# Softmax maximum and sum across partitions: by VectorE in blocks of 32 and one short product each, in place of TensorE transposes

## The chip, the cores and the metric

The kernel runs on one core of a Trainium2 chip. The metric is the device time of the whole kernel in microseconds, lower is better. The four compute engines of the core are named as in the profile: PE (TensorE, matrix products and transposes), DVE (VectorE), ACT (ScalarE) and POOL (GpSimd). Each takes its instructions in order from a queue of its own, and they meet at semaphores. SP (SyncE) issues most of the DMAs.

## The reference, cut to what matters

The kernel computes one post-norm transformer layer in fp32: latent attention over 2048 tokens with 16 heads and a causal mask, then a linear layer, each followed by a layer norm.

```
q     = rms_norm(x @ w_qa.T) @ w_qb.T        # 16 heads, 128 + 64 (rotary)
ckv   = x @ w_kva.T                          # one latent key of 128 + 64 rotary
scores = (q . k) * scale, causal mask
attn  = softmax(scores)                      # max and sum over the keys
x     = layernorm(x + (attn @ v) @ w_o.T)
out   = layernorm(x + (x @ (w * scale).T + bias))
```

## The kernel before

A first phase prepares keys, values and weights (the rows up to about 150 us of the profile). The second phase is the attention, and it is where the change lies.

The 16 heads are worked in four groups of 4 heads, and the 2048 queries in 16 tiles of 128. One iteration `it` is one query tile of one group, so there are 64 iterations. Iteration `it` runs over `keys(it)` = 1 to 16 key tiles, since the mask is causal: 544 steps (it, t) in all, 8.5 on average. One step holds 128 keys on the partitions and 4 heads x 128 queries = 512 columns. So the keys lie across the partitions, and the maximum and the sum over the keys have to cross them.

A step does this, by engine:

- PE `scores`: 5 products of 512 columns into one of two score banks in PSUM (L1464).
- DVE `masked` (t = 0, L1847) or ACT `copy_scores` (L1606) and DVE `max_of` (L1858): the scores go to a slot of a ring in SBUF, the running maximum over the steps to `top`, in SBUF.
- When the iteration's steps are through, the maximum crosses the partitions: PE `turn_max` (4 transposes of 128x128, L1473), DVE `reduce_max` (L1866), PE `spread_max` (4 transposes of a broadcast column, L1484) into the bank `MAXES`.
- DVE `shift` (L1873) subtracts the maximum, ACT `exp` (L1611), ACT `hi` (L1618) rounds to a first part, POOL `values_lo` (L1730) makes the rest, and PE `values` multiplies by the values (3 products, L1494, L1495, L1497).
- DVE `add_up` adds the exponentials into the bank `TOTAL` in PSUM: a copy at t = 0 (L1882, 64 times), an addition otherwise (L1885, 480 times). Then ACT `copy_sum` (L1630), PE `turn_sum` (4 transposes, L1505), DVE `reduce_sum` (L1889) and a reciprocal (L1892), PE `spread_sum` (4 transposes, L1513), DVE `normalise` (L1897).
- ACT `o_hi` (L1636), POOL `o_lo` (L1735), PE `project_out` (step `y`, 12 products, L1527), DVE `add_y` (L1836).

Beside that, each of 32 pairs of iterations has three groups of 18 products of 256 columns: `q` twice (L1427) and `pe` once (L1440), with readers `q_hi`, `q_lo` (L1589, L1829), `rope` (L1808, L1812) and `round_pe` (POOL L1703, L1709), and the DMAs `store_pe` and `load_pe` on SP. PE's results for `q`, `pe`, `y`, the turns and `spread_sum` share three banks in rotation (`aux`).

The order of work is written out ahead by `plan()`: `timetable()` gives every step a slot number and a phase in it, the steps are sorted, `waits_for` pulls prerequisites forward, and every engine runs its part of that one list in order. A slot is one key step, with 13 phases. `scores` of step n come in slot n, its `values` in slot v = `value_slot`, at least 6 slots after the last score of the iteration. In the last quarter of the steps the FFN's steps are mixed in (POOL L1747 to L1768, PE L1535, L1547, DVE L1902 to L1941).

Of the kernel before, what the change touches and what calls it, by code (L numbers as in the profile page):

```python
# [662 lines left out]
N_SCORES, N_AUX = 2, 3  # L663
# [105 lines left out]

def timetable():  # L770

    for it in range(N_ITER):
        for t in range(keys(it)):
            n, v = number(it, t), value_slot(it, t)
            yield n, SCORES_AT, ("scores", it, t)
            yield n, MAX, ("max", it, t)
            yield v - 3, SHIFT, ("shift", it, t)
            yield v - 2, EXP, ("exp", it, t)
            yield v - 1, ROUND, ("hi", it, t)
            yield v - 1, ROUND, ("sum", it, t)  # L780
            yield v - 1, ROUND, ("lo", it, t)
            yield v, VALUES, ("values", it, t)
        e = last_value(it)
        yield last_slot(it) + 1, USE_AT, ("turn_max", it)
        yield value_slot(it, 0) - 3, SPREAD, ("spread_max", it)
        yield e, COPIES, ("copy_sum", it)
        yield e + 1, COPIES, ("copy_out", it)
        yield e, USE_AT, ("turn_sum", it)
        yield e + 3, USE_AT, ("spread_sum", it)
        yield e + 5, USE_AT, ("y", it)  # L790
    for s in range(-2, N_PAIR):
# [3 lines left out]
        for j, use in enumerate(uses):  # L795
            at = window_slot(s, j) if s or use[0] == "pe" else -1
            if s == -1 and use[0] == "pe":
                at = 4
            yield at, USE_AT, use
            if use[0] == "pe":  # L800
                late = 3
                yield at + late, READ, ("round_pe", s + 2)
                yield at + late + 1, READ, ("store_pe", s + 2)
                yield max(at + late + 2, FIRST[2 * s + 2] if s >= 0 else at + 5), READ, ("load_pe", s + 2)


def ffn_timetable():
# [3 lines left out]
    for u in range(NT):  # L811
# [6 lines left out]
        yield n + 1, FFN_TURN, ("turn", u)  # L818
        yield n + 2, FFN, ("scale", u)
        yield n + 3, FFN, ("add_bias", u)  # L820
        yield n + 4, FFN_LINEAR, ("linear", u)
        yield n + 5, MAX, ("z_statistics", u)
# [5 lines left out]
def readers(use):  # L828
# [9 lines left out]
    if use[0] == "turn_max":  # L838
        return [("reduce_max", use[1])]
    if use[0] == "turn_sum":  # L840
        return [("reduce_sum", use[1])]
    if use[0] == "spread_sum":
        return [("normalise", use[1]), ("o_hi", use[1]), ("o_lo", use[1])]
# [15 lines left out]

def waits_for(step):  # L860
# [9 lines left out]
    elif what == "max":  # L870
        yield ("scores", it, *rest)
        if number(it, *rest) >= RING:
            yield ("lo", *previous(it, *rest, RING))
            yield ("sum", *previous(it, *rest, RING))
        if rest[0] == 1 and it >= 2:
            yield ("turn_max", it - 2)
    elif what == "spread_max":
        yield ("reduce_max", it)
# [10 lines left out]
    elif what == "sum":  # L889
        yield ("exp", it, *rest)  # L890
        if it and rest[0] == 0:
            yield ("copy_sum", it - 1)
# [10 lines left out]
    elif what == "copy_sum":  # L903
        yield ("sum", *last_tile(it))
        if it:
            yield ("turn_sum", it - 1)
    elif what == "turn_max":
        yield ("max", *last_tile(it))
    elif what == "reduce_max":
        yield ("turn_max", it)  # L910
        if it >= 8:
            yield ("spread_max", it - 8)
    elif what == "turn_sum":
        yield ("copy_sum", it)
    elif what == "reduce_sum":
        yield ("turn_sum", it)
        if it >= 2:
            yield ("spread_sum", it - 2)
    elif what == "spread_sum":
        yield ("reduce_sum", it)  # L920
# [96 lines left out]
AUX_USES = ("q", "pe", "y", "turn_max", "turn_sum", "spread_sum", "turn", "linear")  # L1017


def plan():  # L1020
# [69 lines left out]
def attention_phase(nc, m, block, x, bias, out):  # L1090


    with ExitStack() as ctx:
# [12 lines left out]
        top = sb("top", [P, 2, 512])  # L1106
        total = sb("total", [P, 512])
# [4 lines left out]
        stats = m.small[:, 20:20 + 8 * HG].rearrange("p (b h) -> p b h", b=8)  # L1112
        sums = sb("sums", [P, 4, HG])
# [5 lines left out]
        z = [unused_table[:, 0:HID], unused_table[:, HID:2 * HID], top[:, 0, :], top[:, 1, :]]  # L1119
# [10 lines left out]
        SCORES, AUX = m.bank[0:N_SCORES], m.bank[N_SCORES:N_SCORES + N_AUX]  # L1130
        OUT, MAXES, TOTAL = m.bank[5:8]
# [13 lines left out]
        max_turned = sem("max_turned")  # L1145
# [9 lines left out]
        sum_copied = sem("sum_copied")  # L1155
        sum_turned = sem("sum_turned")
        sum_done = sem("sum_done")
# [47 lines left out]
        def by_head(view):  # L1205

            return view.rearrange("p (h n) -> p h n", h=HG)

# [176 lines left out]
        def _(pe):  # L1385
            def wait_read(u):
# [7 lines left out]
                elif u[0] == "turn_max":  # L1394
                    pe.wait_ge(max_done, u[1] + 1)
                elif u[0] == "turn_sum":
                    pe.wait_ge(sum_done, u[1] + 1)
# [69 lines left out]
            def turn_max(it):  # L1467
                u = ("turn_max", it)
                shared(u)
                pe.wait_ge(scores_maxed, finished(it))  # L1470
                source = slot(number(it, 0)) if keys(it) == 1 else top[:, it % 2, :]
# [4 lines left out]
            def spread_max(it):  # L1476
                if it:

                    pe.wait_ge(shifted, finished(it - 1))
# [552 lines left out]
```

## Time and profile before

| what | value |
|---|---|
| device time, three runs | 1714.2, 1715.77, 1716.36 us, median 1715.77 |
| span of the profiled execution | 1714.7 us |
| median of the runs less that span | 1.1 us |
| PE busy | 1679.9 us, 98% |
| DVE busy | 1380.5 us, 81% |
| ACT busy | 1120.8 us, 65% |
| POOL busy | 979.7 us, 57% |

The profile gives the profiled execution as its span from the first to the last instruction, and no device time of its own beside it. Busy time of a group is the union of its instructions from start to end. Neighbouring instructions of one engine overlap in their tails, so what one of them costs its engine is read from the distance between starts, in the timeline or in the chain.

### The profile page before, as it was taken

The numbers are of one execution on the slowest core, as the hardware profiler recorded it, in microseconds if no ns is written. First come the engines' busy times: TensorE is split into PE (matmuls) and PEld (weight loads), VectorE is DVE, ScalarE is ACT, GpSimd is POOL, SyncE is SP. The second block draws the span as 40 slices with busy tenths as digits, with TensorE's granted clock in tenths as the row PEclk, the third lists the DMA queues.
The fourth block names the chain that finished last, engine by engine and source line by source line (L and its number), as shares of the span: only waits on it lengthen the run. The fifth ranks groups of instructions, "written<-read, shape, count | busy, mean of one in ns | idle before, by whom it ended". The sixth has DMA issues, their size and how long they took to land.

```text
span 1714.7 us, 28541 instructions
## 1 busy us (share of the span) xinstructions
PE 1679.9 (98%) x8789; PEld 1395.8 (81%) x8789; DVE 1380.5 (81%) x2493; ACT 1120.8 (65%) x2128; POOL 979.7 (57%) x937
## 2 busy tenths in 40 slices
PE   7999999999999999999999999999999999999997
PEld 5567888888888888888888888888888888888775
DVE  3665788888888887878788888888888888888984
ACT  3564676666666676666677666766667777676774
POOL 4333465565555555655566555555556665556785
PEclk9999999999999999999999999999999999999999
DMA  7984322212321412223211413123123111111422
GB/s 204 367 330 136 105 68 62 87 56 88 110 80 37 144 36 81 69 80 117 81 62 44 142 50 92 51 80 114 62 66 105 56 57 62 50 44 44 136 92 80
DMA packets 112175, 164.03 MB, mean 96 GB/s; under 512 B 13600, under 2 KB 83488, under 8 KB 109984
## 3 DMA queue, kind: packets, MB, share of 16 engines
q1 hardware_dynamic: 105296, 125.86, 22.9%
q0 software_dynamic: 4864, 16.26, 3.0%
q10 hardware_dynamic: 1872, 20.19, 2.9%
q8 instruction: 68, 1.11, 0.3%
q14 instruction: 75, 0.61, 0.1%
HBM read 101.19 MB, written 61.08 MB: 95 GB/s over the span
## 4 chain that ended last, share of the span: by engine, by line
PE 89%; POOL 3%; DVE 3%; issue 2%; DMA 1%; ACT 1%; DVEq 0%; SPq 0%; ACTq 0%; POOLq 0%
PE rows L1464 35%; PE bank L1494 7%; PE bank L1497 7%; PE bank L1495 7%; PE rows L1527 7%; PE rows L1427 5%; PE bank L1527 3%; PE rows L392 2%; PE rows L1440 2%; PE bank L1427 2%; PE bank L1484 2%; PE bank L1440 1%; POOL split_p L1730 1%; PE rows L1473 1%; PE rows L1505 1%
## 5 line engine op out<-in xcount | busy, mean ns | idle before, releaser
L1730 POOL TENSOR_TENSOR split_p<-pool,split_p 128x512 fp32r<-128x512 f32 x544 | 703.3, 1294 | 503.2 <-ACT split_p L1618 503.1
L1464 PE MATMUL rows<-q_c,key_c 128*128 128x512 f32 x1632 | 477.0, 400 | 1.4 <-DVE top L1858 1.4
L1606 ACT COPY pool<-rows 128x512 f32<-128x512 f32 x480 | 281.8, 587 | 227.3 <-PE rows L1464 226.6
L1858 DVE TENSOR_TENSOR top<-rows,top 128x512 f32<-128x512 f32 x420 | 288.6, 687 | 124.5 <-ACT pool L1606 121.0
L1873 DVE TENSOR_TENSOR pool<-bank,pool 128x512 f32<-128x512 f32 x544 | 369.7, 680 | 19.8 <-PE bank L1484 19.8
L1611 ACT ACTIVATE pool<-pool 128x512 f32<-128x512 f32 x544 | 345.9, 636 | 18.1 <-DVE pool L1873 17.1
L1618 ACT CAST split_p<-pool 128x512 fp32r<-128x512 f32 x544 | 333.2, 612 | 16.7 <-PE bank L1497 16.7
L1464 PE MATMUL rows<-q_pe,key_pe 128*128 128x512 f32 x1088 | 337.1, 391 | 0.4 <-DMA q_pe<-pe_dram 0.4
L1885 DVE TENSOR_TENSOR bank<-bank,pool 128x512 f32<-128x512 f32 x480 | 330.9, 689 | 0.0
L1464 PEld LDWEIGHTS rows<-q_c,key_c 128*128 128x128 f32 x1632 | 288.0, 189 | 50.0 <-DVE top L1858 5.0
L1464 PEld LDWEIGHTS rows<-q_pe,key_pe 128*128 128x128 f32 x1088 | 204.2, 188 | 46.2 <-DMA q_pe<-pe_dram 0.9
L1497 PE MATMUL bank<-split_p,val 128*128 128x512 f32 x544 | 213.7, 393 | 2.9 <-POOL split_p L1730 2.7
L1494 PE MATMUL bank<-split_p,val 128*128 128x512 f32 x544 | 214.0, 393 | 1.5 <-ACT o_sum L1624 1.0
L1495 PE MATMUL bank<-split_p,val 128*128 128x512 f32 x544 | 212.3, 390 | 0.0
L1527 PE MATMUL rows<-wo,o_t 128*128 128x512 f32 x528 | 127.3, 390 | 0.4 <-ACT o_t L1636 0.4
L1497 PEld LDWEIGHTS bank<-split_p,val 128*128 128x128 f32 x544 | 102.1, 188 | 29.0 <-POOL split_p L1730 7.4
L1494 PEld LDWEIGHTS bank<-split_p,val 128*128 128x128 f32 x544 | 102.1, 188 | 25.9 <-ACT o_sum L1624 3.4
L1735 POOL TENSOR_TENSOR o_t<-o_sum,o_t 128x512 fp32r<-128x512 f32 x64 | 83.0, 1296 | 69.8 <-ACT o_t L1636 69.8
L1495 PEld LDWEIGHTS bank<-split_p,val 128*128 128x128 f32 x544 | 102.2, 188 | 21.2
L1527 PEld LDWEIGHTS rows<-wo,o_t 128*128 128x128 f32 x528 | 98.9, 188 | 21.7 <-issue 1.2
L1636 ACT CAST o_t<-o_sum 128x512 fp32r<-128x512 f32 x64 | 39.7, 621 | 111.4 <-DVE o_sum L1897 97.2
L1427 PE MATMUL rows<-cq,wq 128*128 128x256 f32 x612 | 80.1, 285 | 0.3 <-DVE key_pe L611 0.3
(193 smaller groups left out, 2101.9 us busy)
## 6 DMA issues: line engine op xcount, KB each, us to landing
q_pe<-pe_dram SPq DMA_DIRECT2D x128, 128.0 KB, 2.6
y_dram<-y SPq DMA_DIRECT2D x62, 256.0 KB, 2.1
cq<-cq_dram SPq DMA_DIRECT2D x19, 768.0 KB, 4.9
y<-y_dram SPq DMA_DIRECT2D x48, 256.0 KB, 3.0
pe_dram<-by_sin SPq DMA_DIRECT2D x32, 256.0 KB, 2.1
pe_dram<-by_cos SPq DMA_DIRECT2D x32, 256.0 KB, 2.2
cq_more<-cq_dram SPq DMA_DIRECT2D x10, 768.0 KB, 4.9
table<-table_dram SPq DMA_DIRECT2D x56, 128.0 KB, 2.7
```

The lines of the kernel that those rows point to most:

```text
L1464: mm = pe.matmul(by_head(out), k, q, start=(z == 0), stop=(z == 4))
L1494: pe.matmul(OUT, m.val[:, 0, j, :], split_p[:, n % 2, 0, :], start=(t == 0), stop=False)
L1495: pe.matmul(OUT, m.val[:, 1, j, :], split_p[:, n % 2, 0, :], start=False, stop=False)
L1497: pe.matmul(OUT, m.val[:, 0, j, :], split_p[:, n % 2, 1, :], start=False, stop=(t == keys(it) - 1)).then_inc(values_done, 1)
L1527: mm = pe.matmul(aux(u), o_t[:, a, h * P:h * P + P], m.wo[:, b, h, :], start=(n == 0), stop=(n == 3 * HG - 1))
L1606: nc.scalar.copy(slot(n), SCORES[n % N_SCORES]).then_inc(scores_copied, 1)
L1611: nc.scalar.activation(slot(n), slot(n), ACT.Exp).then_inc(exp_done, 1)
L1618: nc.scalar.copy(split_p[:, n % 2, 0, :], slot(n)).then_inc(p_hi, 1)
L1730: nc.gpsimd.tensor_tensor(split_p[:, n % 2, 1, :], slot(n), stored(split_p[:, n % 2, 0, :]), ALU.subtract).then_inc(p_lo, 1)
L1858: nc.vector.tensor_tensor(out, SCORES[n % N_SCORES], slot(number(it, 0)) if t == 1 else out, ALU.max).then_inc(scores_maxed, 1)
L1873: nc.vector.tensor_tensor(slot(n), MAXES, slot(n), ALU.add).then_inc(shifted, 1)
L1885: nc.vector.tensor_tensor(TOTAL, TOTAL, slot(n), ALU.add).then_inc(summed, 1)
```

## The change

The maximum over the partitions is now taken so: DVE `reduce_max` reduces each 32x32 block of `top` with a transposing reduction (`apply_transpose=True`) to [128 x 16], DVE spreads the 16 numbers to 64 columns by a product with a 0/1 table `quadrant`, PE `fold_max` multiplies these 64 columns by a 0/1 matrix `fold` (one fp32 product, into `aux`), DVE `join_max` reduces the four blocks, and DVE `spread_max` writes `MAXES` by a blockwise transpose of the broadcast result. The sum goes the same way: DVE `reduce_sum` (transposing reduction of `TOTAL`), PE `fold_sum` (one product of 16 columns), DVE `spread_sum` (reciprocal, then a blockwise transpose into `aux`), DVE `normalise`. `copy_sum` on ACT and the 16 transposes of an iteration on PE are gone. `TOTAL` lies in SBUF, the first addition of an iteration takes two slots (so the copy at t = 0 is gone, except in the 4 iterations with one key tile), the bank that is free becomes a third score bank, and `top` has one buffer. All steps get new places in the list, in units of one thirteenth of a slot. A small `fold` table is made once at the start of the attention.

```diff
-N_SCORES, N_AUX = 2, 3
+N_SCORES, N_AUX = 3, 3
+AT = {'scores': -2, 'max': 7.85, 'shift': -36, 'exp': -22, 'hi': -14, 'sum': -7.75, 'lo': -7.65, 'values': 1, 'reduce_max': 20, 'fold_max': 38, 'join_max': 46, 'spread_max': -26, 'reduce_sum': 1, 'copy_out': 10, 'fold_sum': 38, 'spread_sum': 38, 'normalise': 33.1, 'o_hi': 51, 'o_lo': 49.25, 'y': 76, 'add_y': 60.15, 'q': 9, 'q_hi': 45.85, 'q_lo': 20.1, 'pe': 6, 'rope': 19.85, 'round_pe': 63, 'store_pe': 58, 'load_pe': 66}
...
-            yield n, SCORES_AT, ("scores", it, t)
-            yield n, MAX, ("max", it, t)
-            yield v - 3, SHIFT, ("shift", it, t)
-            yield v - 2, EXP, ("exp", it, t)
-            yield v - 1, ROUND, ("hi", it, t)
-            yield v - 1, ROUND, ("sum", it, t)
-            yield v - 1, ROUND, ("lo", it, t)
-            yield v, VALUES, ("values", it, t)
...
-        yield e + 5, USE_AT, ("y", it)
+            for what in ("scores", "max"):
+                yield 13 * n + AT[what], 0, (what, it, t)
+            for what in ("shift", "exp", "hi", "sum", "lo", "values"):
+                yield 13 * v + AT[what], 0, (what, it, t)
...
-    for n, phase, step in itertools.chain(timetable(), ffn_timetable()):
+    for n, phase, step in itertools.chain(timetable(), ((13 * n + phase, 0, step) for n, phase, step in ffn_timetable())):
         at.setdefault((n, phase), []).append(step)
-        for reader in readers(step):
-            at.setdefault((n + 1, READ), []).append(reader)
...
-        top = sb("top", [P, 2, 512])
-        total = sb("total", [P, 512])
+        top = sb("top", [P, 512])
+        TOTAL = sb("total", [P, 512])[:, :]
+        fold = sb("fold", [P, P])
...
-        SCORES, AUX = m.bank[0:N_SCORES], m.bank[N_SCORES:N_SCORES + N_AUX]
-        OUT, MAXES, TOTAL = m.bank[5:8]
+        SCORES, AUX = [m.bank[0], m.bank[1], m.bank[5]], m.bank[2:5]
+        OUT, MAXES = m.bank[6:8]
...
-                for h in range(HG):
-                    mm = pe.transpose(aux(u)[:, h * P:h * P + P], source[:, h * P:h * P + P], m.ident[:, :])
-                mm.then_inc(max_turned, 1)
+                pe.wait_ge(max_widened, it + 1)
+                pe.matmul(aux(u)[:, 0:16 * HG], fold[:, :], wide_max[:, it % 2, :], start=True, stop=True
+                          ).then_inc(max_folded, 1)
...
+                pe.wait_ge(sum_reduced, it + 1)
+                pe.matmul(aux(u)[:, 0:4 * HG], fold[:, :], row_sum[it % 2], start=True, stop=True).then_inc(sum_folded, 1)
...
+                nc.vector.tensor_reduce(part_max[:, it % 2, :], in_blocks(source), AX.X, ALU.max, apply_transpose=True
+                                        ).then_inc(max_reduced, 1)
+                dve.wait_ge(max_reduced, it + 1)
...
+                nc.vector.tensor_tensor(wide_max[:, it % 2, :].rearrange("p (a b) -> p a b", a=4),
...
+                nc.vector.tensor_reduce(stats[:, it % 8, :],
...
+                nc.vector.transpose(in_blocks(MAXES),
+                                    stats[:, it % 8, :].rearrange("p (b n) -> p b n", n=1).broadcast_to([P, 4 * HG, 32])
+                                    ).then_inc(max_spread, 1)
...
+                if keys(it) == 1:
                     nc.vector.tensor_copy(TOTAL, slot(n)).then_inc(summed, 1)
+                elif t == 1:
+                    nc.vector.tensor_tensor(TOTAL, slot(n - 1), slot(n), ALU.add).then_inc(summed, 1)
+                elif t > 1:
+                    dve.wait_ge(summed, sums_made(it, t) - 1)
                     nc.vector.tensor_tensor(TOTAL, TOTAL, slot(n), ALU.add).then_inc(summed, 1)
...
+                nc.vector.reciprocal(inv_sum[it % 2], aux(u)[:, 0:4 * HG]).then_inc(inv_done, 1)
+                dve.wait_ge(inv_done, it + 1)
+                nc.vector.transpose(in_blocks(aux(u)),
+                                    inv_sum[it % 2].rearrange("p (b n) -> p b n", n=1).broadcast_to([P, 4 * HG, 32])
+                                    ).then_inc(sum_spread, 1)
```

## Rows read from the trace of the kernel before

**Rows 1.** The page: span, busy time, PE's granted clock in 40 slices.

```profile
span 1714.7 us, 28541 instructions
PE 1679.9 (98%) x8789; PEld 1395.8 (81%) x8789; DVE 1380.5 (81%) x2493; ACT 1120.8 (65%) x2128; POOL 979.7 (57%) x937
PEclk9999999999999999999999999999999999999999
```

**Rows 2.** Windows over the attention, 200 to 1600 us: sum of busy times.

```profile
sum 1400.00, PE 1399.39 PEld 1189.98 DVE 1181.29 ACT 943.41 POOL 817.13; mean PE 349.85 PEld 297.49 DVE 295.32 ACT 235.85 POOL 204.28
```

**Rows 3.** The chain that ended last, 1560 to 1617 us: start, us, what.

```profile
1561.67 0.44 PE rows L1513 x4
1562.11 1.16 PE rows L1464 x5
...
1565.77 2.72 PE bank L1527 x12
...
1575.28 2.15 PE rows L1427 x18
```

**Rows 4.** Timeline of PE in the preparation: start, us, engine, group.

```profile
105.97 1.00 PE L402 MATMUL bank<-pool,x_t 128*128 128x64 f32 x8
106.81 1.08 PE L459 MATMUL bank<-pool 128*128 128x512 f32 x2
```

**Rows 5.** Timeline of DVE and POOL in the attention, 800 to 812 us.

```profile
803.41 1.29 POOL L1730 TENSOR_TENSOR split_p<-pool,split_p 128x512 fp32r<-128x512 f32 x1 [0.98 <-ACT split_p L1618]
803.53 0.69 DVE L1885 TENSOR_TENSOR bank<-bank,pool 128x512 f32<-128x512 f32 x1
...
804.73 0.68 DVE L1873 TENSOR_TENSOR pool<-bank,pool 128x512 f32<-128x512 f32 x1
...
805.33 0.68 DVE L1882 COPY bank<-pool 128x512 f32<-128x512 f32 x1
...
808.31 0.68 DVE L1889 TENSOR_REDUCE sums<-bank 128x4 f32<-128x512 f32 x1
...
809.02 0.18 DVE L1892 RECIPROCAL sums<-sums 128x4 f32<-128x4 f32 x1
...
809.12 0.68 DVE L1858 TENSOR_TENSOR top<-rows,top 128x512 f32<-128x512 f32 x1
...
811.54 0.74 DVE L1812 TENSOR_TENSOR by_sin<-rows,table 128x256 f32<-128x256 f32 x2
```

**Rows 6.** Groups by form, whole span: busy us, mean ns, idle before.

```profile
L1730 POOL TENSOR_TENSOR split_p<-pool,split_p 128x512 fp32r<-128x512 f32 x544 | 703.3, 1294 | 503.2 <-ACT split_p L1618 503.1
...
L1885 DVE TENSOR_TENSOR bank<-bank,pool 128x512 f32<-128x512 f32 x480 | 330.9, 689 | 0.0
...
L1882 DVE COPY bank<-pool 128x512 f32<-128x512 f32 x64 | 43.7, 683 | 0.0
```

**Rows 7.** Waits, 200 to 1600 us: who waited, total us, times, longest us.

```profile
POOL split_p L1730 <- ACT split_p L1618: 486.3, 456, 5.4
...
DVE top L1858 <- ACT pool L1606: 130.7, 192, 3.1
```

**Rows 8.** Timeline of DVE and POOL in the preparation, two places.

```profile
43.25 0.72 POOL L309 TENSOR_TENSOR small<-small 128x2 f32<-128x2 f32 x1 [4.87 <-DVE small L621]
...
43.71 0.36 DVE L637 TENSOR_TENSOR k_rot<-t_cos,t_sin 128x64 f32<-128x64 f32 x2
...
124.89 1.04 POOL L321 TENSOR_TENSOR ffn_rows<-ffn_rows,small 128x512 f32<-128x512 f32 x1
...
125.18 0.97 DVE L637 TENSOR_TENSOR k_rot<-t_cos,t_sin 128x64 f32<-128x64 f32 x2
```

**Rows 9.** Line 637 (DVE, preparation): duration ns min/median/max.

```profile
L637 DVE TENSOR_TENSOR k_rot<-t_cos,t_sin x32: 210/222/1716, 22.0 to 138.1; 128x64 f32<-128x64 f32 x32
```

**Rows 10.** Windows near the end, with the FFN's steps mixed in.

```profile
1620.00:1640.00 20.00, 17.95 (x88) 13.47 (x87) 18.34 (x41) 16.66 (x29) 18.82 (x33) 1.00 0.28 93
1640.00:1660.00 20.00, 18.25 (x94) 14.84 (x93) 17.40 (x41) 16.72 (x30) 18.36 (x32) 1.00 0.34 106
```

More of the change, by code:

```diff
@@ L798, in timetable @@
                 at = 4
-            yield at, USE_AT, use
+            yield 13 * at + AT[use[0]], 0, use
+            if use[0] == "q":
+                yield 13 * at + AT["q_hi"], 0, ("q_hi", *use[1:])
+                yield 13 * at + AT["q_lo"], 0, ("q_lo", *use[1:])
             if use[0] == "pe":
[L801 to L804, printed above, removed]
+                yield 13 * at + AT["rope"], 0, ("rope", s + 2)
+                yield 13 * at + AT["round_pe"], 0, ("round_pe", s + 2)
+                yield 13 * at + AT["store_pe"], 0, ("store_pe", s + 2)
+                yield max(13 * at + AT["load_pe"], 13 * (FIRST[2 * s + 2] if s >= 0 else at + 5) + READ), 0, ("load_pe", s + 2)
 def ffn_timetable():
@@ L837, in readers @@
         return [("rope", use[1])]
[L838 to L843, printed above, removed]
+    if use[0] == "fold_max":
+        return [("join_max", use[1])]
+    if use[0] == "fold_sum":
+        return [("spread_sum", use[1]), ("normalise", use[1])]
     if use[0] == "y":
@@ L857, in last_tile, with sum_of, sums_made @@
     return it, keys(it) - 1
+def sum_of(it, t):
+    return it, 1 if t == 0 and keys(it) > 1 else t
+def sums_made(it, t):
+    return sum(keys(n) - (keys(n) > 1) for n in range(it)) + t + (keys(it) == 1)
 def waits_for(step):
@@ L873, in waits_for @@
             yield ("lo", *previous(it, *rest, RING))
-            yield ("sum", *previous(it, *rest, RING))
-        if rest[0] == 1 and it >= 2:
-            yield ("turn_max", it - 2)
+            yield ("sum", *sum_of(*previous(it, *rest, RING)))
+        if rest[0] == 1 and it:
+            yield ("reduce_max", it - 1)
     elif what == "spread_max":
-        yield ("reduce_max", it)
+        yield ("join_max", it)
         if it:
@@ L902, in waits_for @@
             yield ("o_lo", it - 2)
[L903 to L907, printed above, removed]
-        yield ("max", *last_tile(it))
-    elif what == "reduce_max":
-        yield ("turn_max", it)
+    elif what == "reduce_max":
+        yield ("max", *last_tile(it))
+        if it >= 2:
+            yield ("fold_max", it - 2)
+    elif what == "fold_max":
+        yield ("reduce_max", it)
+    elif what == "join_max":
+        yield ("fold_max", it)
         if it >= 8:
             yield ("spread_max", it - 8)
-    elif what == "turn_sum":
-        yield ("copy_sum", it)
     elif what == "reduce_sum":
-        yield ("turn_sum", it)
+        yield ("sum", *last_tile(it))
         if it >= 2:
-            yield ("spread_sum", it - 2)
+            yield ("fold_sum", it - 2)
+    elif what == "fold_sum":
+        yield ("reduce_sum", it)
     elif what == "spread_sum":
-        yield ("reduce_sum", it)
+        yield ("fold_sum", it)
     elif what == "normalise":
@@ L1016 @@
 PROJECTION_STEPS = [("q", N_PAIR - 1, 0), ("q", N_PAIR - 1, 1)]
-AUX_USES = ("q", "pe", "y", "turn_max", "turn_sum", "spread_sum", "turn", "linear")
+AUX_USES = ("q", "pe", "y", "fold_max", "fold_sum", "turn", "linear")
 def plan():
@@ L1896, in normalise @@
                 dve.wait_ge(out_copied, it + 1)
-                nc.vector.tensor_tensor(o_sum[:, it % 2, :], aux(("spread_sum", it)), o_sum[:, it % 2, :], ALU.mult
+                nc.vector.tensor_tensor(o_sum[:, it % 2, :], aux(("fold_sum", it)), o_sum[:, it % 2, :], ALU.mult
                                         ).then_inc(normalised, 1)
@@ L1966, in _ @@
                     reduce_max(*at)
+                elif what == "join_max":
+                    join_max(*at)
+                elif what == "spread_max":
+                    spread_max(*at)
                 elif what == "shift":
@@ L1972, in _ @@
                     reduce_sum(*at)
+                elif what == "spread_sum":
+                    spread_sum(*at)
                 elif what == "normalise":
```

163 lines of the change are left out of this document (85 added, 78 removed).

## Prediction, made before the changed kernel ran

> **What bounds the kernel now.** I read the page first. PE is busy 98% of 1714.7 us, DVE 81%, POOL 57%, and PE's granted clock is at its upper level, 2.4 GHz, in every slice, so no time lies in the clock [rows 1]. Then the windows over the attention: between 200 and 1600 us PE is busy 1399.4 of 1400 us, DVE 1181 (84%), POOL 817 (58%) [rows 2]. A busy PE need not be a PE at its peak, so I asked the chain what stands in it and how long each group holds PE up to the start of the next: five score products 1.16 us, twelve of `y` 2.72, eighteen of `q` 2.15, four transposes 0.44 [rows 3]. The reader is to see that the chain goes from one PE group straight into the next. The waits say the same from the other side: POOL waits for ACT and DVE's maximum waits for a copy of scores that PE has only just made (130.7 us) [rows 7]. PE sets the time of the attention, and a microsecond taken from its list is one off the end, until another engine is full.
>
> **PE's list before.** 544 steps of 8 products at about 0.227 (2.72/12): 990 us; 64 `y` at 2.72: 174; 96 groups of `q` and `pe` at 2.15: 206; 256 groups of four transposes at 0.44: 113. Together 1483 us. The busy time of the transposes would make more of them (union of their tails), the distance between starts is what counts.
>
> **What leaves PE, what comes.** All 256 groups of transposes go: -113 us. 128 fp32 products of 64 or 16 columns come. Nearest is the fp32 product of 64 columns in the preparation: eight of them start 105.97 and the next group 106.81, 0.105 us each [rows 4], so +13 us. Bounds: not less than that row (16 columns may be a little less, nothing that counts), at most a 512-column product of 0.227, 29 us. I take 13. PE's list becomes 1384 us, 99 less, and 1714.7 - 99 = 1616 us is the time if PE remains full; 1631 with the upper price.
>
> **What comes to DVE.** Its passes of 512 columns start 0.60 us apart (804.73, 805.33); two of 256 take 0.74 with the tail, so 0.33 apart, which makes about 1.05 ns an element and 0.06 fixed [rows 5]. After a reduction the reciprocal that needs its result starts 0.71 later, so such a wait for the own result costs 0.11; the reciprocal itself 0.10. Before: 1632 passes for mask or maximum, shift and sum, 320 for the two reductions, `normalise`, `add_y` and `q_lo`, and 32 of `rope`: 1984 x 0.60 = 1190, 64 halves at 0.33 = 21, 64 x 0.21 = 13: 1224 us of the attention's 1483, 83%, which the 84% of the windows bears out. The change:
>
> - 60 of 64 copies at t = 0 go [rows 6]: -36 us.
> - Two block transposes per iteration, to `MAXES` and into `aux`: no row shows one. Nearest is the copy of 512 columns into a bank, 0.60 apart [rows 5]: 128 x 0.60 = +77. Bound below: the same, since 512 columns have to be written; above: twice the per-element part, 1.14 each.
> - The two reductions are there before and after; the transposing form I price at the plain 0.60, same bounds, 0 to +0.54 each.
> - The product with `quadrant` and `join_max`, 64 columns each: 0.06 + 64 x 1.05 ns = 0.13, 128 of them: +17.
> - Three more waits for the own result per iteration (product after reduction, transpose after reciprocal, `normalise` after transpose): 192 x 0.11 = +21.
>
> Sum +79, DVE's list 1303 us. Against PE's 1384 that is 94%: it fits, with 81 us to spare. ACT loses 64 copies and gets nothing. That is the cover under which all of DVE's additions cost nothing, and it is thin.
>
> **The running sum in SBUF.** The 480 additions read a bank and a slot before; now they read two SBUF operands. Is that free? The preparation has one such instruction, L637, 128x64 from two SBUF tiles. It takes 222 ns at the median and up to 1716 [rows 9]. At 125.18 it stands beside a POOL product of 128x512 from 124.89 to 125.93, and the two of the pair take 0.97 in place of 0.36: the first ends when POOL's does. Beside a POOL operation of 2 columns it isn't lengthened [rows 8]. So a two-SBUF addition waits here for a large POOL operation to end, and presumably POOL for it. The Trainium skill has this as a rule (SBUF — State Buffer, section "SBUF: two separate sides"): a VectorE operation with two SBUF inputs and a GpSimd operation that reads SBUF exclude each other for the whole instruction. The trace agrees in the long rows of L637, and not at 43.71.
>
> What it costs, w per addition: below, 0. Above, the place of before: the addition starts 0.12 after a POOL operation of 1.29 [rows 5], 1.17 to wait. Met at random, POOL busy 58% of the time with half of 1.25 left: 0.36. But the two also order each other. `shift` and `max` between two additions take 1.20, a POOL operation 1.25, so once POOL's has been held back by an addition it fits into that gap, and the next addition waits 0.05. Here the new places matter: `hi` moves from the phase -8 to -14, a half slot earlier against `lo` and `sum` (-7.65, -7.75, as before), so POOL has its next operand in hand when an addition ends, and is held rather than holding. Any extra piece in DVE's queue (about one per step: `normalise`, `add_y`, `q_lo`, a reduction) spoils the pattern once. Half the additions at 0.36, half at 0.05 makes 0.20; since at 95% load not all of DVE's idle time is of use, I take 0.25.
>
> DVE's list is then 1303 + 480 w, against PE's 1384. It fits up to w = 0.17. Beyond, the time is 1616 + 480 (w - 0.17), and it is that of before at w = 0.375. With 0.25: +38 us.
>
> **Third score bank.** PE may now be three steps ahead of the maximum, not two. In stretches of plain steps PE needs 1.82 us per step and DVE 1.80 + w, in the slots with `q` or `y` 2 to 3 us more; the third bank lets DVE fall back in the plain ones and recover. I price it at no gain of its own: it is what makes an average load of 94% usable at all.
>
> **Moved steps and added waits.** `add_y` at 60.15 pulls `y` (76) to the same place: DVE stands behind `add_y` while PE runs 2.72 us of `y`, with `shift` and `sum` queued behind it and `exp` behind those. If DVE is 2.7 us late by then, as at such a load it mostly is, this costs nothing; if it is not, it makes it so, once. `join_max` stands 8 phases behind `fold_max`, more than a microsecond of cover; `fold_sum`, `spread_sum` and `normalise` fall on one place (33.1), where DVE waits for one product, 0.27 at most, if it is not late. `q` to `q_lo` and `pe` to `rope` keep their distance (11 and 14 phases for 11). `round_pe` is pulled to 58 (46 before), `store_pe` is at 58 for 59 and `load_pe` on SP at 66 for 72, all wanted slots later. The fold table is three small operations, once. Together 0.
>
> **The end.** From 1620 to 1660 POOL is busy 37.2 of 40 us [rows 10], with DVE at 89%. There every addition of 0.53 that makes POOL wait goes on the path: about 15 steps, at most 8 us, I take 6.
>
> Sum: 1714.7 - 113 + 13 + 38 + 6 = 1659, and 1.1 for the median of the runs: 1660 us.
>
> **Rivals.**
>
> 1. *The exclusion costs nothing or hides* (w below 0.17, by synchrony or because it holds only now and then, as at 43.71). PE stays full: 1612 to 1631. For it: POOL's and DVE's 1.25 and 1.20; against: nine extra pieces per iteration. 0.24.
> 2. *DVE becomes the bound through POOL.* This is the rule of the page above, taken in full, and the one mechanism that makes the kernel slower. It decides from w = 0.375. At 0.5, 1616 + 158 = 1774; at 0.82, 1928; if every addition met POOL as at 803.53, 2096. For it: POOL busy 58%, random meeting is 0.36 already. Against: `hi` earlier, and each wait shifts the two against each other. 0.18.
> 3. *32-block operations run at half speed.* 256 x 0.54 = 138 us more on DVE: 1441, and PE's 1384 no longer bounds: 1673 with w = 0, 1793 with 0.25. By the skill (Vector Engine (DVE) Microarchitecture Reference, "The reshape front-end and per-opcode configuration") the transposing array keeps one element per cycle; no run here shows it yet. 0.09, half of it on each side of before.
> 4. *The turn of fold and join, or `add_y`, holds PE*: DVE waits for `y`, then everything is late by 2.3 us in each of 64 iterations with nothing left to recover it, +147: 1763. Against: being late removes the wait. 0.03.
>
> **Numbers.** My case (w from 0.17 to 0.37, 1622 to 1712) has 0.46, with a range of its own of 1630 to 1700. 0.2%, 3.4 us, is about what can be told from no change here. Faster: 0.46 + 0.24 + half of case 3 = 0.74; slower: 0.18 + 0.04 + 0.03, less a sliver around equality, 0.23; same 0.03. The range goes from 1612, where PE is full at the low price, up to 1745, w = 0.44: it leaves out the upper part of cases 2 to 4.
>
> **What would show it.** PE: L1473, L1484, L1505, L1513 gone, 128 short products at 0.10 to 0.23, PE's busy share in the middle a few points below 100%. DVE: new block operations at 0.60 apart (0.68 long); if they are 1.2 long, case 3. L1885's successor has a median near 0.65 but a mean of 0.85 to 0.95 with a tail up to 1.8; a mean near 0.65 is case 1, above 1.05 case 2. POOL's L1730 grows too, by up to 0.55. If the additions are all short and PE is still not full, the cause is one I don't name. The prediction is wrong if w lies outside 0.17 to 0.37.

## The result: 1729.0 us, 0.8% slower than before

The changed kernel takes 1729.0 us (median of four runs, 1727.2 to 1731.7) against 1716.1 (four runs beside them, 1714.2 to 1717.3). The ratio is 1.008, with a 95% interval of 1.0068 to 1.0093. Forecast were 1660 us and "faster" with 0.74. The range of 1612 to 1745 holds the time, the sign is wrong.

The page of the kernel after:

```profile
span 1725.5 us, 27198 instructions
PE 1626.0 (94%) x8021; PEld 1336.1 (77%) x8021; DVE 1588.2 (92%) x2692; ACT 1123.4 (65%) x2064; POOL 1061.8 (62%) x937
DVE  3566999999999999999999999999999999999995
PEclk9999999999999999999999999999999999999899
```

And its windows from 200 to 1600 us, in the columns of [rows 2]:

```profile
sum 1400.00, PE 1345.57 PEld 1128.25 DVE 1365.58 ACT 943.96 POOL 888.23; mean PE 1345.57 PEld 1128.25 DVE 1365.58 ACT 943.96 POOL 888.23
```

PE had 0.6 us without work in these 1400 us [rows 2], now it has 54. DVE went from 1181 to 1366: 97.5%. PE has lost its transposes and DVE has become the engine that sets the time. POOL has 71 us more with the same instructions.

Groups of DVE and POOL, after (busy us, mean ns, idle before):

```profile
L1896 DVE TENSOR_TENSOR total<-total,pool 128x512 f32<-128x512 f32 x420 | 391.0, 931 | 0.0
L1893 DVE TENSOR_TENSOR total<-pool 128x512 f32<-128x512 f32 x60 | 59.1, 985 | 0.0
L1716 POOL TENSOR_TENSOR split_p<-pool,split_p 128x512 fp32r<-128x512 f32 x544 | 776.1, 1432 | 382.2 <-ACT split_p L1612 378.7
L1858 DVE TENSOR_TENSOR wide_max<-part_max,small 128x64 f32<-128x64 f32 x64 | 35.3, 552 | 2.2
L1853 DVE TRANSPOSE_TENSOR_REDUCE part_max<-top 128x16 f32<-128x512 f32 x60 | 41.9, 699 | 0.0
L1875 DVE STREAM_TRANSPOSE bank<-stats 128x512 f32<-128x512 f32 x64 | 45.5, 712 | 0.2
L1903 DVE TRANSPOSE_TENSOR_REDUCE sums<-total 128x16 f32<-128x512 f32 x64 | 44.7, 698 | 0.0
L1911 DVE STREAM_TRANSPOSE rows<-sums 128x512 f32<-128x512 f32 x44 | 32.0, 727 | 1.5
```

The addition took 689 ns [rows 6]. It now takes 931, and the first one of an iteration, from two slots, 985. So w, the forecast's name for the time that an addition waits, is (420 x 0.242 + 60 x 0.296)/480 = 0.249 us on average, where 0.25 was forecast. POOL's `values_lo` grew from 1294 [rows 6] to 1432. All four block operations are within 0.05 us of a plain pass (0.68 [rows 5]). But the product with `quadrant`, 64 columns, takes 552 ns.

One line's own durations (min/median/max), after, say what kind of lengthening it is:

```profile
L1896 DVE TENSOR_TENSOR total<-total,pool x420: 671/683/1835, 185.0 to 1665.2; 128x512 f32<-128x512 f32 x140
```

More than half the additions take what they always took; a minority takes up to 1.15 us more. The timeline, after, shows one of each kind:

```profile
805.19 0.69 DVE L1896 TENSOR_TENSOR total<-total,pool 128x512 f32<-128x512 f32 x1
...
805.85 1.30 POOL L1716 TENSOR_TENSOR split_p<-pool,split_p 128x512 fp32r<-128x512 f32 x1 [0.51 <-ACT split_p L1612]
...
1597.19 1.29 POOL L1716 TENSOR_TENSOR split_p<-pool,split_p 128x512 fp32r<-128x512 f32 x1 [1.20 <-ACT split_p L1612]
...
1597.67 1.37 DVE L1896 TENSOR_TENSOR total<-total,pool 128x512 f32<-128x512 f32 x1
```

At 805.19 the addition ends as POOL starts: no loss. At 1597.67 it starts while POOL is in its operation (to 1598.48) and ends 0.56 after that, at 1599.04. Additions start 0.60 apart where none waits [rows 5], so it did its work only when POOL was through.

The waits changed sides, after, 200 to 1600 us (total us, times, longest):

```profile
POOL split_p L1716 <- ACT split_p L1612: 360.4, 307, 3.5
ACT pool L1605 <- DVE pool L1883: 141.8, 152, 3.0
PE bank L1504 <- POOL split_p L1716: 25.6, 20, 2.2
PE rows L1525 <- ACT o_t L1624: 9.0, 9, 1.8
```

Before, the largest of DVE's waits was for ACT (130.7 [rows 7]). Now ACT's `exp` waits for DVE's `shift`, and PE, at the end of the line `shift`, `exp`, `hi`, `lo`, for POOL's part.

### The profile page after: what moved, and what is told of

It is laid out like the page before. It is cut to its first block and busy times, and to the rows that moved or that the text cites. A ratio compares the mean times of both kernels' runs of the same rounds, so it can differ in the third digit from the quotient of the medians.

```text
span 1725.5 us, 27198 instructions
## 1 busy us (share of the span) xinstructions
PE 1626.0 (94%) x8021; PEld 1336.1 (77%) x8021; DVE 1588.2 (92%) x2692; ACT 1123.4 (65%) x2064; POOL 1061.8 (62%) x937
## 5 line engine op out<-in xcount | busy, mean ns | idle before, releaser
L1716 POOL TENSOR_TENSOR split_p<-pool,split_p 128x512 fp32r<-128x512 f32 x544 | 776.1, 1432 | 382.2 <-ACT split_p L1612 378.7
L1896 DVE TENSOR_TENSOR total<-total,pool 128x512 f32<-128x512 f32 x420 | 391.0, 931 | 0.0
L1483 PE MATMUL rows<-q_c,key_c 128*128 128x512 f32 x1089 | 314.5, 397 | 0.2 <-DVE top L1843 0.2
L1600 ACT COPY pool<-rows 128x512 f32<-128x512 f32 x320 | 185.9, 581 | 82.3 <-PE rows L1483 81.4
L1483 PEld LDWEIGHTS rows<-q_c,key_c 128*128 128x128 f32 x1089 | 200.0, 190 | 36.9 <-DVE top L1843 0.6
L1483 PE MATMUL rows<-q_pe,key_pe 128*128 128x512 f32 x726 | 226.4, 393 | 1.0 <-DMA q_pe<-pe_dram 1.0
L1843 DVE TENSOR_TENSOR top<-rows,top 128x512 f32<-128x512 f32 x283 | 192.0, 679 | 9.2 <-ACT pool L1600 9.0
L1483 PEld LDWEIGHTS rows<-q_pe,key_pe 128*128 128x128 f32 x726 | 137.6, 190 | 31.5 <-DMA q_pe<-pe_dram 1.4
L1483 PE MATMUL bank<-q_c,key_c 128*128 128x512 f32 x543 | 156.3, 396 | 0.0
L1600 ACT COPY pool<-bank 128x512 f32<-128x512 f32 x160 | 92.9, 581 | 44.2 <-PE bank L1483 43.7
L1502 PEld LDWEIGHTS bank<-split_p,val 128*128 128x128 f32 x544 | 104.0, 191 | 18.9
```

Of the source, the lines that this page charges most:

```text
L1483: mm = pe.matmul(by_head(out), k, q, start=(z == 0), stop=(z == 4))
L1502: pe.matmul(OUT, m.val[:, 1, j, :], split_p[:, n % 2, 0, :], start=False, stop=False)
L1600: nc.scalar.copy(slot(n), SCORES[n % N_SCORES]).then_inc(scores_copied, 1)
L1716: nc.gpsimd.tensor_tensor(split_p[:, n % 2, 1, :], slot(n), stored(split_p[:, n % 2, 0, :]), ALU.subtract).then_inc(p_lo, 1)
L1843: nc.vector.tensor_tensor(out, SCORES[n % N_SCORES], slot(number(it, 0)) if t == 1 else out, ALU.max).then_inc(scores_maxed, 1)
L1896: nc.vector.tensor_tensor(TOTAL, TOTAL, slot(n), ALU.add).then_inc(summed, 1)
```

## The experiments

Three theories stood at the start. A: additions and POOL's operations exclude each other, and this makes DVE the bound. B: an addition that reads what the addition before wrote is slow by itself. C: the new places or the added waits of the list cost the time. All times are medians of four or five runs, each beside runs of the kernel before with medians of 1714.2 to 1716.1 us. Two theories that came later, F and G, are told in the expectations of e11.

| kernel | edit | us | ratio to before, 95% |
|---|---|---|---|
| after | | 1729.0 | 1.008, 1.0068 to 1.0093 |
| e1 | POOL's `lo` covers 32 of 512 columns | 1655.6 | 0.965, 0.9633 to 0.9665 |
| e2 | sum in PSUM, two score banks | 1726.4 | 1.006, 1.0044 to 1.0078 |
| e3 | two score banks alone | 1771.6 | 1.032, 1.0303 to 1.0337 |
| e2b | sum in PSUM, 3 score and 2 shared banks | 1690.6 | 0.986, 0.9839 to 0.9872 |
| e6 | product with `quadrant` on ACT | 1702.1 | 0.992, 0.9904 to 0.9937 |
| e7b | e2b and e6 together | 1677.7 | 0.978, 0.9768 to 0.98 |
| e5 | `hi` late, as before | 1764.4 | 1.029, 1.0273 to 1.0307 |
| e9 | e7b with `hi` late | 1683.6 | 0.982, 0.9803 to 0.9836 |
| e10 | e7b, `add_y` behind `y` | 1679.1 | 0.979, 0.9776 to 0.9809 |
| e4 | kernel before, sum in SBUF | 1780.1 | 1.038, 1.0363 to 1.0397 |
| e11 | additions of 32 columns | 1666.2 | 0.972, 0.9704 to 0.9731 |
| e12 | e11, short products twice | 1685.1 | 0.982, 0.981 to 0.9837 |

**e1, a short POOL operation.** It leaves out most of the second part of the exponentials.

```diff
-nc.gpsimd.tensor_tensor(split_p[:, n % 2, 1, :], slot(n), ...
+w = 512 if n < 2 else 32
+nc.gpsimd.tensor_tensor(split_p[:, n % 2, 1, 0:w], slot(n)[:, 0:w], ...
```

> The changed kernel, but GpSimd's remainder of each key step covers 32 of 512 columns from the third step on (the other columns keep the remainders of the first two steps, so the output is a little off). It tells whether the long additions come from GpSimd. Theory A (a VectorE addition of two SBUF operands waits while a large GpSimd operation runs, and that made VectorE the bound): the 420 additions fall from a mean of 931 ns to 675 to 700, the product with the quadrant table from 552 to 225, VectorE's work between starts falls from about 1480 us to 1325, below TensorE's 1384, and the time falls to 1620 to 1655; up to 35 us of that can come from GpSimd itself near the end, so the step 500 (1535 us now) should come 60 to 85 us earlier. Theory B (the additions are long because they read what the one before wrote to SBUF): mean stays 900 to 950 and step 500 stays within 10 us. Theory C (the new places of the steps hold TensorE, not VectorE's load): additions short, but step 500 within 15 us of now.

Measured: 1655.6 us, 73.5 less than after. The groups of DVE in e1:

```profile
L1897 DVE TENSOR_TENSOR total<-total,pool 128x512 f32<-128x512 f32 x420 | 322.4, 768 | 0.0
L1894 DVE TENSOR_TENSOR total<-pool 128x512 f32<-128x512 f32 x60 | 43.0, 716 | 0.0
L1859 DVE TENSOR_TENSOR wide_max<-part_max,small 128x64 f32<-128x64 f32 x64 | 15.8, 247 | 2.2
```

DVE's instructions are the same as in after, and only POOL's were made shorter: additions, first additions and the small product all shorten, which refutes B. The small product goes from 552 to 247 ns. The additions stay above the 675 to 700 that were expected, and the time is just outside the expected range. Not all of the 73.5 us is DVE's: POOL itself is no longer late either, and PE's 25.6 us of waits for `split_p` are gone.

**e2, e3 and e2b, the banks.** The sum goes back to PSUM (e2), with the score banks that are then left; the banks alone (e3); and with a third score bank at the cost of a shared one (e2b). The edits in short:

```diff
 e2:  TOTAL = m.bank[5]; SCORES = m.bank[0], m.bank[1]; N_SCORES = 2
 e3:                     SCORES = m.bank[0], m.bank[1]; N_SCORES = 2
 e2b: TOTAL = m.bank[3]; SCORES = m.bank[0], [1], [5]; AUX = m.bank[2], [4]
```

> The changed kernel with the running sum back in a PSUM bank and two score banks in place of three; everything else, the new places too, stays. Theory A: 420 additions at 690 ns, only the 60 first ones (two slots in SBUF) stay long; VectorE's work falls by 105 to 115 us to about 1370, and TensorE's 1384 bounds: 1635 to 1675. Theory B: the same here. Theory C: 1715 to 1740, since the places are unchanged. If the third bank is what allows such a load, the time lies above 1690 with short additions.

> The changed kernel with two score banks in place of three and nothing else changed. Theory A: VectorE bounds either way, so only the swings between plain steps and steps with other work are buffered less: 1732 to 1750. If the third bank mattered much more than I priced it (nothing): 1760 or more. If it is worthless: 1725 to 1731.

> The changed kernel with the running sum in a PSUM bank, three score banks kept, and two shared banks in place of three. With two score banks and the sum in PSUM TensorE waited 56 us for the maximum before a score product (between 200 and 1590 us), VectorE's additions were short, and the time was 1726. If those two are separate causes (theory A plus a real price of the third score bank), both are gone here: 1655 to 1685, as far as two shared banks suffice; each use of one must wait for the reader of the last but one, and if that is late TensorE stands before q, pe or y: then 1690 to 1730 with these waits in place of the others. Theory C (the places): 1715 to 1735.

Measured: 1726.4, 1771.6 and 1690.6. From e3 to e2 only the place of the sum differs: it is worth 45 us. From e3 to after only the third score bank differs: 42.5 us. From e2 to e2b a shared bank becomes a score bank: 36 us. In e2 and e2b the 420 additions of L1896 have a mean of 688 ns; here is e2b's line:

```profile
L1896 DVE TENSOR_TENSOR rows<-rows,pool 128x512 f32<-128x512 f32 x420 | 289.0, 688 | 0.0
```

The 60 first ones still read two slots and take 1140 and 1094. The time of e2 lies outside what A forecast (1635 to 1675) and inside what C did (1715 to 1740). It is e2b, with the same new places, that speaks against C, and it too comes out 6 us above the range that was expected of A. What the third bank does shows in PE's waits in e3, 200 to 1590 us:

```profile
PE rows L1483 <- DVE top L1843: 61.8, 61, 2.5
PE rows L1483 <- DVE pool L1833: 12.0, 18, 1.2
PE bank L1504 <- POOL split_p L1716: 6.1, 12, 0.7
```

With two banks PE waits 74 us for a maximum or a mask, to have a bank for the next scores. In after these waits are 0.2 us. So with two score banks the change is no gain even where the 420 additions don't meet POOL (e2): it needs the third bank. To have it the kernel moved the sum to where it meets POOL. As e2b shows, a shared bank could have been given up instead.

**e6 and e7b, the product with `quadrant`.** Four ACT operations of 16 columns make it instead, each with a column of `quadrant` as its scale.

The cut leaves out the waits and DVE's old product, and writes 16 for `4 * HG`:

```diff
+def widen_max(it):          # step at 30, on ACT
+    ...
+    for a in range(4):
+        nc.scalar.activation(wide_max[:, it % 2, 16 * a:16 * a + 16], part_max[:, it % 2, :],
+                             ACT.Copy, scale=quadrant[:, a:a + 1])
```

> The changed kernel, but the product with the quadrant table is made by ScalarE in four small operations. VectorE loses 64 operations of 0.48 us between starts (0.13 was my price). Theory A, VectorE the bound: 31 us less work, 1695 to 1712. If VectorE's load is not what sets the time: 1724 to 1732.

> As the run with three score and two shared banks, and the product with the quadrant table made by ScalarE in four small operations (it has 35% idle), in place of one VectorE operation of two SBUF operands. Theory A: 64 x 0.5 us less on VectorE; if VectorE is near the bound 5 to 25 us less than that run, if TensorE is full 0 to 5.

Measured: 1702.1, 26.9 us less than after. What left DVE is 35.3 us of busy time, or some 64 x 0.46 = 29 us between starts. A microsecond of DVE is then nearly one of the end. On top of e2b, where DVE is no longer full, the same edit gives 12.9. Together (e7b) it is 1677.7, the best version, 2.2% faster than before. Its page:

```profile
PE 1611.3 (96%) x8021; PEld 1331.1 (79%) x8021; DVE 1464.9 (87%) x2628; ACT 1164.9 (70%) x2320; POOL 991.7 (59%) x937
```

POOL's `values_lo` is back at a mean of 1320 ns.

**e5 and e9, the earlier `hi`.**

```diff
-'hi': -14,
+'hi': -8.3,
```

> The changed kernel with hi at phase -8.3, where it was before, in place of -14, so GpSimd gets its operand just as VectorE comes to its addition. My ordering argument says that the wait grows from 0.28 us towards the 0.41 of the run that moved only the sum: 1745 to 1800. If the place of hi doesn't matter, within 5 us of 1729.

> The run with three score and two shared banks, the sum in PSUM and the product on ScalarE (1677.7 us), with hi at -8.3 in place of -14. In the changed kernel this move cost 35 us, and two ways lead there: the longer waits of the additions for GpSimd (1021 ns for 931), or GpSimd's remainder coming late for the value products (57 us of TensorE's waits). Theory A (the exclusion): without additions of two SBUF operands the move costs 0 to 8 us. If lateness alone did it: 20 to 40.

Measured: +35.4 us on after, +5.9 on e7b. Groups and waits of e5:

```profile
L1896 DVE TENSOR_TENSOR total<-total,pool 128x512 f32<-128x512 f32 x420 | 428.9, 1021 | 0.0
```

```profile
PE bank L1504 <- POOL split_p L1716: 57.1, 66, 2.4
```

w is (420 x 0.332 + 60 x 0.147)/480 = 0.31 with `hi` late, 0.25 with `hi` early. The same move is worth six times as much where additions and POOL exclude each other. Lateness alone doesn't do it: in e9, with `hi` as late, PE waits only 4.4 us for POOL's part:

```profile
PE bank L1508 <- POOL split_p L1730: 4.4, 10, 1.1
```

So the earlier `hi` does what the forecast's argument on order said, and it doesn't cause the loss.

**e10, `add_y` behind `y`.**

```diff
-'y': 76, 'add_y': 60.15
+'y': 60.15, 'add_y': 72
```

> The same base (1677.7 us), with the place of y given openly as 60.15, where add_y had pulled it, and add_y at 72, about one step later, so VectorE doesn't stand behind add_y while TensorE runs y (37 us of waits between 200 and 1590 us). I priced that wait at nothing, since a late VectorE recovers it: 1674 to 1681 then. If it costs where VectorE is at 90%: 1660 to 1672. If two shared banks make a later reader worse: 1682 to 1695.

Measured: 1679.1, 1.4 more than e7b, inside the error. Yet the wait itself is gone. The first fence is e7b, the second e10, 200 to 1590 us:

```profile
DVE y L1836 <- PE rows L1529: 25.4, 23, 4.0
DVE y L1836 <- PE bank L1529: 11.9, 10, 1.8
```

```profile
DVE y L1836 <- PE rows L1529: 8.4, 9, 2.7
```

28 us of DVE's waiting for `y` are gone (1.0 us more are left on PE's other bank), and nothing is gained. But DVE's idle time as a whole hardly fell, from 101.8 to 99.7 of 1390 us: it waits 13 us more for ACT's copies of scores and 7 us for the DMA of `y` instead. So e10 shows that this place is not what costs, not that 28 us of DVE's time are worth nothing. With e2b, where all new places stand, faster than before, this refutes C as the main cause.

**e4, the sum in SBUF on the kernel before.** Of the rest of the change it has only the single buffer for the maximum, to make room.

```diff
-OUT, MAXES, TOTAL = m.bank[5:8]
+OUT, MAXES = m.bank[5:7]
+TOTAL = top[:, 1, :]     # the maximum keeps one buffer
```

> The kernel before with its running sum in SBUF and nothing else moved (the maximum gets one buffer in place of two to make room). Theory A: with the old places an addition starts just after GpSimd's remainder, so the additions have a mean of 1000 to 1400 ns; VectorE's work is 1224 us plus 480 waits: at a wait of 0.54 us it passes TensorE's 1483. I expect a wait of 0.45 to 0.8 and 1720 to 1810 us. Theory B: additions of 900 to 950 ns and a time of 1714 to 1722, with TensorE full.

Measured: 1780.1, 64.8 more than before. Groups of e4:

```profile
L1886 DVE TENSOR_TENSOR top<-top,pool 128x512 f32<-128x512 f32 x480 | 521.1, 1086 | 0.0
```

w is 0.40 in the old order, a little less than the 0.45 to 0.8 expected, and the time is in the expected range. The single buffer is not seen to cost: in e4's waits DVE doesn't wait for `turn_max`, and PE waits 1.2 us for the maximum ahead of it. This run says most about the failed step, below.

**e11 and e12, what is left.** In e11 the additions from the third key tile on cover 32 columns and leave out the rest of the sum, in e12 each short product is issued twice as well.

```diff
-nc.vector.tensor_tensor(TOTAL, TOTAL, slot(n), ALU.add)
+nc.vector.tensor_tensor(TOTAL[:, 0:32], TOTAL[:, 0:32], slot(n)[:, 0:32], ALU.add)
+pe.matmul(...)           # e12: once more ahead of fold_max's and of fold_sum's
```

> This leaves out most of the running sum: the 420 additions from the third key tile on cover 32 of 512 columns. DVE loses some 420 x 0.57 = 240 us of work, and with it nearly all that holds POOL. What is left is PE's own list with the new places and waits. Theory F (the remaining distance to 1631 us in the versions so far is DVE's load alone): with DVE near 80% PE has no idle time left and the time is 1631 us, or 1616 if the short fp32 products cost 0.105 us as in the forecast. Theory G (the new places, or the hand-over from PE to DVE and back for the maximum, cost PE time by themselves): the time stays at 1650 us or more with PE below 98% in the attention, as in the version with the short POOL operation (1655.6).

> On top of the version with short additions every one of the 128 short fp32 products (64 or 16 columns) is issued twice, with the same result. If PE sets the time, the difference to that version is the price of the products themselves: at 0.105 us each +13 us, at 0.23 us each +29 us. If PE has idle time to give (theory G), it is below 10 us.

Measured: 1666.2 and 1685.1. Windows of e11 and e12, 200 to 1590 us:

```profile
200.00:1590.00 1390.00, 1361.25 (x6779) 1150.67 (x6777) 1288.32 (x2247) 970.54 (x1736) 853.65 (x708) 0.99 0.24 79
```

```profile
200.00:1590.00 1390.00, 1368.88 (x6948) 1163.24 (x6947) 1270.85 (x2204) 952.67 (x1706) 834.14 (x676) 0.99 0.24 77
```

e11 came out on G's side, but it separates F and G less than planned: DVE fell to 93%, not to 80%. The reason is in one line of e11 (duration ns min/median/max) and in its timeline:

```profile
L1896 DVE TENSOR_TENSOR total<-total,pool x420: 167/594/1321, 183.5 to 1605.9; 128x32 f32<-128x32 f32 x140
```

```profile
800.99 1.29 POOL L1716 TENSOR_TENSOR split_p<-pool,split_p 128x512 fp32r<-128x512 f32 x1 [0.95 <-ACT split_p L1612]
801.06 1.30 DVE L1858 TENSOR_TENSOR wide_max<-part_max,small 128x64 f32<-128x64 f32 x1
```

An addition of 32 columns can take 0.17 us, and half of them take 0.59 or more. A product of 64 columns that starts 0.07 behind POOL ends 0.08 behind it, 1.30 later. The wait does not shrink with the DVE instruction; it is what is left of POOL's. What remains of PE's idle time in e11, 28.8 of 1390 us, stands in PE's waits:

```profile
PE bank L1501 <- ACT o_sum L1618: 11.8, 6, 3.0
...
PE rows L1525 <- POOL o_t L1721: 5.9, 3, 2.0
...
PE bank L1504 <- POOL split_p L1716: 4.4, 6, 1.1
```

These are hand-overs of `copy_out`, `o_lo` and `lo`, a few long ones each. Before, PE's idle time in 1400 us was 0.6.

e12 less e11 is 18.9 us, while PE's idle time fell by 7.6 (28.8 to 21.1). So 128 more short products are an estimated 26.5 us of PE's list, 0.21 each.

## Why the prediction was wrong, point by point

**The step that failed** is the one that turns w into time: "It fits up to w = 0.17. Beyond, the time is 1616 + 480 (w - 0.17), and it is that of before at w = 0.375." w was 0.249, as forecast, and the kernel is slower all the same. That w came out so well is in part luck: the mixture gave 0.20, and 0.25 was taken for the load in general. The step behind it failed, and three things are wrong in it.

1. *It takes two lists that fit on average to fit in time.* e4 shows it with none of the change's other parts but the single buffer. DVE's list there is 1224 + 480 x 0.40 = 1416 us, PE's 1483; by the step it costs nothing. It cost 64.8 us. e1, e11 and e7b have DVE at 95, 93 and 93% of 1390 us, and PE is 26 to 29 us idle; but there PE's waits are hand-overs, not shown to come from additions. A single addition waits up to 1.15 us. That two or three banks and two buffers of `split_p` don't carry PE over such waits is a reading of this, not shown: no run varied the depth of `split_p`.
2. *DVE's list was too short.* The product with `quadrant` was priced at 0.13 by its columns. It reads two SBUF operands, as the additions do, and waits for POOL as they do: 0.55 long, some 0.46 apart with a tail of 0.09 as for a pass (0.69 long, 0.60 apart). That is 64 x 0.33 = 21 us more than the price. e6, where the whole product leaves DVE (64 x 0.46 = 29 us), bears it out with 26.9. The four block operations are together 0.12 us longer than four plain passes (0.712 + 0.698 + 0.699 + 0.727 - 4 x 0.68): 7 us. So the list is 1303 + 120 + 21 + 7 = 1451 us, not 1423.
3. *PE's list was too short.* [Rows 4] has eight records, and the prediction took them for eight products. They are four. After has 102 + 26 records of L1492 for 64 products:

```profile
L1492 PE MATMUL rows<-wide_max,fold x102: 217/273/473, 175.4 to 1616.0; 128*128 128x64 f32 x102
L1492 PE MATMUL bank<-wide_max,fold x26: 217/273/421, 217.3 to 1609.8; 128*128 128x64 f32 x26
```

An fp32 product has two records, so [rows 4] gives 0.84/4 = 0.21, and e12 gave 0.21. The starts in the trace of after agree:

```profile
1594.88 0.33 PE L1492 MATMUL bank<-wide_max,fold 128*128 128x64 f32 x2
1594.99 0.19 PEld L1501 LDWEIGHTS bank<-split_p,val 128*128 128x128 f32 x1
1595.02 0.48 PE L1501 MATMUL bank<-split_p,val 128*128 128x512 f32 x1
...
1595.33 0.40 PE L1502 MATMUL bank<-split_p,val 128*128 128x512 f32 x1
```

From the start of the short product to the next start it is 0.14, and from there to the one behind it 0.31, where it is 0.23 elsewhere: 0.22 to 0.23 for the short product. With 16 columns the same count gives 0.25. PE's list is 1483 - 113 + 27 = 1397, and a full PE would end at 1629, close to the upper price of the prediction.

**The sum again.** DVE's list of 1451 is 54 above PE's. With DVE never idle the span would be 1714.7 - (1483 - 1451) = 1683. DVE was idle 34 of the 1400 us: 1717. The forecast's 1654 ahead of the end is this same sum with 1423 and no idle time. So 28 us of the miss are DVE's list (point 2) and 34 are its own idle time, which the step puts at nothing (point 1). Point 3 doesn't enter while DVE bounds. The end adds to it. The 520 steps up to 1590 us are only 3 us later than before (`shift` of step 520, counted from 0, at 1588 before, at 1591 after), as this sum has it. The last 24, with the FFN's steps among them, take 80 us from that `shift` to the last one, not 67. That makes 1730. What comes behind the last `shift` is 5 us shorter than before (55 for 60), which makes 1725, against a span of 1725.5.

The windows of the end, first before, then after:

```profile
1600.00:1660.00 60.00, 53.49 (x264) 41.30 (x263) 54.33 (x120) 47.90 (x84) 53.23 (x86) 1.00 0.25 80
```

```profile
1600.00:1660.00 60.00, 46.17 (x189) 35.42 (x190) 55.91 (x114) 39.09 (x68) 46.17 (x67) 0.89 0.17 54
```

DVE is at 93%. PE, now often without work, had a granted clock of 0.89 here, where it was 1.00 before; it was 0.63 from 1604 to 1609, with PE busy 1.60 of 5 us. What this clock costs was not separated. The price forecast for the end was 6 us. In e1, e11 and e7b too these 24 steps take 75 to 76 us, 8 to 9 more than before, with short or shortened additions. So most of it isn't the additions' doing. What it is was not tested.

**The rest of the steps.**

- *What leaves and comes to PE*: the transposes are gone, as forecast; the short products see above.
- *Block operations*: 0.70 to 0.73 us long. Case 3 (half speed) did not occur. Each of the four costs what a pass over 512 columns costs.
- *The exclusion* was read rightly from [rows 8]. As the Trainium skill's rule (SBUF — State Buffer, section "SBUF: two separate sides") says, a VectorE operation with two SBUF inputs and a GpSimd operation that reads SBUF do not run together; the traces of after and e11 agree, at 1597.67 and 801.06. It was applied to one line of the two that it holds for. Rival 2, that DVE becomes the bound through POOL, is what happened. It was given 0.18, with a threshold of w = 0.375; it decided at 0.25. So the mechanism that came was named, with its threshold set too high.
- *Two slips in the numbers*: the forecast's own case runs from 1622, with the 6 us of the end, to 1712, without them, and the upper end of the range (1745 at w = 0.44) is without them too.
- *Order*: w by chance would be 0.36, the forecast's mixture 0.20. The old order gave 0.40 (e4), `hi` late in the new list 0.31 (e5), the new one 0.25.
- *Third score bank*: priced at no gain of its own, it is worth 42.5 us in this kernel (e3). The sentence that it makes a load of 94% usable was right in kind, but then the loss without it is its price, and a load of 94% is not fully usable with it either.
- *Moved steps and added waits*: together 0. e10 bears it out for the place of `add_y`. PE's waits for `copy_out` and `o_lo` are new, and not separated.
- *Case 4* (the turn of fold and join, or `add_y`, holds PE): 4.5 us in 1390, PE's waits for `wide_max`. It did not occur.

**What stays open.** The span of e7b, 1675, is 46 us above the 1629 us of a full PE. PE's idle time from 200 to 1590 us is 27 us, but idle time makes a stall look too short: a product of 512 columns is recorded with 0.39 to 0.40 us and the next one starts 0.23 after it, so the first 0.17 us of a delay lie under the record. I counted the delay of each PE group against its usual distance between the same neighbours, from the first `shift` to that of step 520. It is 7 us before, 90 in after, 64 in e4 and 36 in e7b, where the idle time of the same stretch is 1, 57, 34 and 22. So 29 of the 46 us are such delays, and the rest lies in the last 24 steps and what follows them. The largest of PE's waits in e7b is 10.5 us for `copy_out`; whether its place, ACT's or DVE's lateness causes it wasn't tried. In e7b the 60 first additions still read two slots and have a mean of 1158 ns, 28 us above a plain one.

## What to carry to other kernels

Before an accumulator or a small product is moved to SBUF, count every VectorE instruction that will have two SBUF operands, and price each by what is left of the GpSimd operation that it meets, not by its own columns. That the lists of two engines fit beside each other on average is not yet a time: in e4 the second list was 95% of the first (1416 to 1483), and it cost 65 us. Ask whether the buffers between the two carry the longest single stall, and try a buffer more or less: the third score bank was worth 36 to 42 us here. Of a change in many parts build the parts: here the turn across partitions on VectorE with a third score bank, the sum still in PSUM, was worth 25 us (e2b against before), and with the sum in SBUF, which even frees a third shared bank, it was 38 slower than that (after against e2b).

## What the runs showed of the hardware that was not expected

- A two-SBUF operation of DVE can be lengthened far beyond its own size by POOL. With 32 columns the shortest took 0.17 us and the median 0.59 (e11); with 64 the mean was 0.25 beside short POOL operations (e1) and 0.55 in after; with 512 it was 0.69 before, from a bank, and 0.93 in after. POOL's own operation is lengthened too, 1294 to 1432 ns on average.
- An fp32 product leaves two records in the profile, and at 64 or 16 columns takes 0.21 to 0.25 us of PE ([rows 4], e12, after), about as much as a product of 512 columns of the rounded kind (0.227).
- The transposing reduction and the blockwise transpose of 128x512 fp32, the latter from SBUF to PSUM with a broadcast input, run in 0.70 to 0.73 us, within 0.05 us of a plain pass (0.68 [rows 5]).
